# Scratch rows that hold Q and K side by side, and what is zeroed of them at the start

## The reference

```python
xn = _layernorm(x)
# attention branch (attention over the 16 heads of one token, not over tokens)
q = (ln(xn) @ wq + bq).reshape(b, n, 16, 64)          # k, v likewise
fq = elu(q) + 1.0;  fk = elu(k) + 1.0
kv = einsum('bhnd,bhne->bnde', fk, v)
attn = einsum('bhnd,bnde->bhne', fq, kv) / (fq . fk.sum(heads) + 1e-6)
y1 = xn + attn @ wo + bo
s  = y1 + gelu(ln(y1) @ fc_w + fc_b) @ proj_w + proj_b
# routing branch: 64 slots, top-8 softmax weights alpha per token, slot sums over
# the whole sequence, a GRU and slot attention, then out = alpha @ slot values @ wo
g  = silu(route_and_mix(xn))
x  = x + s * g
```

## Time and profile before

| | us |
|---|---|
| median of two timed runs | 2913.88 (2902.56 and 2925.21) |
| profiled execution, device time | 2816.93 |
| its span on the slowest core (core 7) | 2815.4 |
| spans of the other cores | 2774.6 to 2814.9 |

### The profile page before, as it was taken

The page is one execution under the profiler, slowest core; times in us unless marked ns, Lnnn a source line. Parts: engine busy times, 40 slices in busy tenths (PEclk is TensorE's granted clock), DMA queues, the critical chain, the costliest instruction groups (busy, mean ns, idle before and its releaser), DMA issues. The chain is left out here.

```text
span 2815.4 us, 19258 instructions; the slowest of 8 cores (2774.6 to 2815.4 us)
## 1 busy us (share of the span) xinstructions
PE 1251.0 (44%) x6244; PEld 571.1 (20%) x6244; DVE 653.8 (23%) x1713; ACT 376.9 (13%) x594; POOL 119.8 (4%) x133
## 2 busy tenths in 40 slices
PE   0004343443443332173644726430594976849610
PEld 0002121221221110032222322220242433324200
DVE  0023435345343011212314123120102010020022
ACT  0001111211211000010100101000312304122111
POOL 1000000000000001100000000003000010100000
PEclk9997566666665555585866858765697997979855
DMA  9941011111101643443161441529458092762844
GB/s 186 166 72 57 30 60 42 48 60 47 44 30 19 112 72 53 67 80 70 53 105 53 75 74 49 101 67 143 61 54 126 4 118 58 69 81 22 120 172 164
DMA packets 409766, 217.27 MB, mean 77 GB/s; under 512 B 371203, under 2 KB 375428, under 8 KB 409412
## 3 DMA queue, kind: packets, MB, share of 16 engines
q0 software_dynamic: 182176, 89.49, 26.4%
q1 hardware_dynamic: 227492, 126.55, 16.7%
HBM read 230.00 MB, written 58.72 MB: 103 GB/s over the span
## 5 line engine op out<-in xcount | busy, mean ns | idle before, releaser
L578 PE MATMUL pT<-cIDb,xnb 128*128 128x128 bf16 x512 | 64.8, 307 | 258.4 <-DVEq L191 258.4
L590 PE MATMUL pM<-xnTs,w1ab 128*128 128x512 bf16 x512 | 150.6, 463 | 19.9 <-DVEq L191 17.3
L1764 DVE TENSOR_TENSOR y1t<-pTf,y1t 128x512 f32<-128x512 f32 x32 | 22.1, 691 | 579.0 <-PE pTf L1834 579.0
L1803 PE MATMUL pMa<-h2T,fcwb 128*128 128x512 bf16 x512 | 127.7, 394 | 19.1 <-ACTq L191 19.1
L1803 PE MATMUL pMb<-h2T,fcwb 128*128 128x512 bf16 x512 | 124.4, 387 | 0.0
L1820 PE MATMUL pPb<-g1F,pjcb 128*128 128x512 bf16 x512 | 118.8, 392 | 10.6 <-DMA pjcb<-pjw 10.6
L1820 PE MATMUL pPa<-g1F,pjcb 128*128 128x512 bf16 x512 | 113.1, 379 | 9.1 <-ACTq L191 4.7
L578 PEld LDWEIGHTS pT<-cIDb,xnb 128*128 128x128 bf16 x512 | 49.6, 138 | 274.7 <-issue 274.7
L1787 PE MATMUL pT0d<-cIDb,h2b 128*128 128x128 bf16 x128 | 16.2, 307 | 196.6 <-DVEq L191 139.5
L1388 PE MATMUL pBig<-wqb,xhT 128*128 128x512 bf16 x256 | 75.1, 460 | 50.2 <-ACTq L191 50.2
L639 ACT ACT_TABLE_LOAD x16 | 20.5, 1283 | 489.0 <-PE pM L590 489.0
(11 more groups left out here) (250 smaller groups left out, 1790.2 us busy)
## 6 DMA issues: line engine op xcount, KB each, us to landing
xld<-x8k SPq DMA_DIRECT2D x64, 512.0 KB, 5.2
pjcb<-pjw POOLq DMA_DIRECT2D x32, 1024.0 KB, 10.9
y1scr<-XN SPq DMA_DIRECT2D x4, 2048.0 KB, 6.8
y1t<-y1scr SPq DMA_DIRECT2D x4, 2048.0 KB, 10.3
fcwb<-fcw POOLq DMA_DIRECT2D x32, 256.0 KB, 18.9
sscr<-y1t SPq DMA_DIRECT2D x4, 2048.0 KB, 12.7
xre<-x8k SPq DMA_DIRECT2D x16, 512.0 KB, 4.8
sre<-sscr SPq DMA_DIRECT2D x16, 512.0 KB, 5.7
```

What stands on the lines that cost most here:

```text
L578: i = t.transpose(pT0[:, cc * 128:(cc + 1) * 128], xb[:, cc * 128:(cc + 1) * 128], cIDb[:])
L590: i = t.matmul(dstp[:, 0:512], w1ab[:, cc * 512 + ch * 128: cc * 512 + (ch + 1) * 128], xnTs[:, cc * 512:(cc + 1) * 512], start=(cc == 0), ...
L1764: i = v.tensor_tensor(y1v(mt).rearrange("p (s w) -> p s w", s=4)[:, :, d * 128:(d + 1) * 128], pTf[:, :].rearrange("p (s w) -> p s w", s=4 ...
L1803: i = t.matmul(dstp[:, :], fcwb[:, m * 1024 + cc * 128: m * 1024 + (cc + 1) * 128], h2T[:, cc * 512:(cc + 1) * 512], start=(cc == 0), stop ...
```

## The change

1. The two tensors `scr_q` and `scr_k`, (4, 8192, 128) each, become one, `scr_qk`, of 32776 rows of 128 elements. A row holds Q of a token and head in its first 64 elements and K in the other 64. Every half tile of 4096 rows is followed by one spare row.
2. The four copies of zeros become eight of 128 elements each, for the spare rows; `zpad` has 1024 rows.
3. VectorE writes Q and K into `tmb` interleaved by head, 64 elements of one and 64 of the other, and one store carries all 2048 elements of a partition (4096 contiguous bytes). VectorE's first write of a part now waits for that one store of the part before.
4. ScalarE writes V to `AMK` in place of `tmb[:, 0:1024]`, and waits for the store of V of the part before. V's stores count on `ss1`; in `emit_b` VectorE, which is the first to write `AMK` there, waits for the last of them.
5. `FQ2h` is loaded from the start of the rows, `FK2h` from element 64 of the same rows on: what lies in the rows 64 to 127 of the tiles is then no longer zero but K, or Q of the next row. They are not read.

```diff
-        "zpad": np.zeros((32768, 64), dtype=BF),
+        "zpad": np.zeros((1024, 64), dtype=BF),
@@
-    scr_q = nc.dram_tensor("scr_q", [4, 8192, 128], BF16)
-    scr_k = nc.dram_tensor("scr_k", [4, 8192, 128], BF16)
+    scr_qk = nc.dram_tensor("scr_qk", [32776, 128], BF16)
@@ block at L301, GpSimd
-                        for scr in (scr_q, scr_k):
-                            for kk in range(2):
-                                dmx(g, bass.AP(scr, kk * 2097152, [[1, 2097152]]),
-                                    bass.AP(zpad_d.tensor, 0, [[1, 2097152]]),
-                                    swB, 'wB')
+                        for mt4 in range(4):
+                            for half in range(2):
+                                po = (mt4 * 8194 + half * 4097 + 4096) * 128
+                                dmx(g, bass.AP(scr_qk, po, [[1, 128]]),
+                                    bass.AP(zpad_d.tensor, 0, [[1, 128]]),
+                                    swB, 'wB')
@@ emit_a, VectorE
+                            T3 = tmb[:, 0:2048].rearrange("p (h x) -> p h x", h=16)
                             for st in range(4):
                                 v.wait_ge(sac, acS + 3 * st + 1)
-                                if st >= 1:
-                                    v.wait_ge(ss0, s0S + 32 * st)
-                                i = v.scalar_tensor_tensor(
-                                    tmb[:, 0:1024], pBig0[:, :], 1.0, JUNK[:], ...)
+                                v.wait_ge(ss0, s0S + 16 * st)
+                                i = v.scalar_tensor_tensor(
+                                    T3[:, :, 0:64], pBig0 (16 x 64), 1.0, JUNK (16 x 64), ...)
                                 v.wait_ge(sac, acS + 3 * st + 2)
-                                if st >= 1:
-                                    v.wait_ge(ss1, s1S + 16 * st)
-                                i = v.scalar_tensor_tensor(
-                                    tmb[:, 1024:2048], pBig1[:, :], 1.0, JUNK[:], ...)
+                                i = v.scalar_tensor_tensor(
+                                    T3[:, :, 64:128], pBig1 (16 x 64), 1.0, JUNK (16 x 64), ...)
@@ emit_a, ScalarE
-                                a.wait_ge(ss0, s0S + 32 * st + 16)
-                                i = a.activation(tmb[:, 0:1024], pBig0[:, :], AF.Identity)
+                                a.wait_ge(ss1, s1S + 16 * st)
+                                i = a.activation(AMK[:, :], pBig0[:, :], AF.Identity)
@@ emit_a, SyncE, store_st
-                                s.wait_ge(sdv, dvS + 9 + 2 * st)
-                                dmx(s, scr_q [[2048, 128], [128, 16], [1, 64]], tmb[:, 0:1024], ss0, 's0')
                                 s.wait_ge(sdv, dvS + 10 + 2 * st)
-                                dmx(s, scr_k [[2048, 128], [128, 16], [1, 64]], tmb[:, 1024:2048], ss1, 's1')
+                                dmx(s, scr_qk [[2048, 128], [1, 2048]], tmb[:, 0:2048], ss0, 's0')
                                 s.wait_ge(sac, acS + 3 * st + 3)
-                                dmx(s, scr_v ..., tmb[:, 0:1024], ss0, 's0')
+                                dmx(s, scr_v ..., AMK[:, :], ss1, 's1')
@@ transposing loads of both halves
-                                in_=bass.AP(scr_q, ..., [[128, 4096], [1, 128]])   # FQ2h
-                                in_=bass.AP(scr_k, ..., [[128, 4096], [1, 128]])   # FK2h
+                                in_=bass.AP(scr_qk, h, [[128, 4096], [1, 128]])       # FQ2h
+                                in_=bass.AP(scr_qk, h + 64, [[128, 4096], [1, 128]])  # FK2h
@@ emit_b, VectorE
                             v.wait_ge(sld, C['ld'])
+                            v.wait_ge(ss1, s1S)
```

## The result

| us | before | after |
|---|---|---|
| median of the timed runs | 2828.38 (10 runs, lowest 2821.91) | 2692.31 (12 runs, lowest 2680.14) |
| profiled execution (span) | 2816.93 (2815.4) | 2688.01 (2686.5) |
| ratio, 95% interval | | 0.9516 (0.9496 to 0.9536) |

The change is 4.8% faster, 136 us by the medians and 129 us from profiled execution to profiled execution. The median of before moved too: the two runs that were shown ahead of the prediction (2902.56 and 2925.21) turned out to be among the four highest of ten (2883 to 2925), while the other six lie between 2821.91 and 2829.45. In some runs of either kernel the cores of one die show a lower granted clock than the others (0.67 against 0.71 in the changed kernel's run of 2791.91), and the ratios leave these runs out; without them the medians are 2824 and 2687.

The account below looks back on a forecast made before the run. Bound by waits for transfers: zeros before the first barrier, emit_a's stall, emit_b's turn. 93 + 43 - 3 - 3 - 6 = 124 us, taken from the median 2913.88, gives 2790 us; range 2682 to 2825.

Parts of the forecast that it names:

- the same 124: The summed saving of 124 us, subtracted from the median of two timed runs, 2913.88, to give 2790 us.
- stage C: From the first Q matmul of emit_a through the last emit_b and projection; the terms outside the start sum to 31 us.
- The start: At the block at L301, VectorE's first instruction moves from 174.46 to about 81.1 us without the zeros: 93, bounds 78 and 99.
- They cancel: At the start, eight small copies cost about 1.5 us and wvb landing earlier without zeros gains 1.5, leaving 93.
- The stall in `emit_a`: V's copy no longer waits for the store of Q ahead of part 3: 43 us, 34.1 idle and 9 lower clock.
- The margin in part 3: In emit_a, VectorE's Q waits for part 2's joint store but just fits: 0 lost, or 0.8 per tile (-3) with slower transposes.
- VectorE's wait for V's store: In emit_b, VectorE's masks wait until the last V is stored: 0.7 us per tile, -3, range 0 to -6.
- The loads of K: Shifted FK2h loads take 1.5 us longer, counted once per tile at the turn in emit_b: -6, bounds 0 and -12.
- turn: In emit_b, TensorE waits about 20 us per tile for second-half loads and aog's store; a sign expected 20 to 23 us.
- That only the start pays: Rival: emit_a's stall moves to VectorE's Q or K loads lose the gain; 93 + 0 to 15, about 2814, chance 0.24.
- That the zeros weren't what the barrier waited for: Rival: at the start, the barrier did not wait for zeros or wvb lands later; sum 31, 2883 us, chance 0.04.
- The K loads: Rival: two shifted K loads per tile lose 23 us each, or from 16 the kernel is slower at all; chance 0.02.

Follow-up runs that it names:

- V's place alone: The kernel before with only V written to AMK, its store on its own semaphore, and VectorE waiting for the last in emit_b: ratio 0.985, 2794.82 us.
- its repeat: The changed kernel itself, unaltered, timed again on the same chip as the one with unshifted loads of K: ratio 0.957 to the kernel before.
- the first run: The changed kernel with 16 MB of zeros copied again behind wvb in place of the eight small copies: ratio 0.983 to the kernel before.

## Why the prediction was right and wrong

**The time, 2790 forecast, 2692 measured: wrong.** The step that failed is the last of the sum, "I take the same 124 from the median". That median rested on two runs, which ten runs show to be among its four highest, while I had an execution of the same kernel 97 us under both and said that nothing in the trace explained the gap. The other half of that step, 2816.93 - 124 = 2693, is where the changed kernel is: profiled at 2688.01, median 2692.31. The range held that level only because I let it reach down to it. That the sum itself comes so near is in part luck: the start gave 5.6 us more than forecast and stage C 6.1 less. Set against the median that the kernel before really has, my forecast was a change of 38 us, less than a third of what came, although my sum was 124 of the 129 between the two profiled executions.

**The start, 93 forecast, 98.6 measured (97.5 from core 7 to core 5).** The reading was right: the barrier follows the last transfer that GpSimd issued, and moves to the next one. Of the two corrections the one for the eight small copies, 1.5 us, was right. The other was mis-sized, so "They cancel" is the faulty step: without zeros beside it the last piece of `wvb` ended at 73.4 and not at 81.4 (medians of the cores), 8 us earlier where I took 1.5 and bounded at 6. That the barrier follows the last transfer by 1.2 to 1.4 us and not 0.6 takes some of it back.

**The stall in `emit_a`, 43 forecast.** The mechanism was right to the instruction; the tile I had taken apart gained 9.6 us of the 10.0. The size was taken from the core with the longest waits of L1388, 50.2 us. Cores 5 and 2 of the same trace have these rows:

```profile
PE pBig L1388 <- ACTq L191: 40.0, 12, 8.1
...
PE pBig L1388 <- ACTq L191: 45.1, 12, 12.1
```

40.0 is the least of the eight and 45.1 the median. By the same formula, 45.1 - 16.1 = 29 idle and 9 at the lower clock, that is 38. V's place alone shortened stage C by 30.8 over the median of the cores, with its own wait for V's store (about 4) already inside, so 35. Taking one core's waits for all was an error of 5 us; another 3 stay open.

**The margin in part 3.** "It just fits" held: 0.34 us of wait in the tile shown, 1.2 in all on core 5, and 2 on the average of the cores (5.5 at most).

**VectorE's wait for V's store, -3.** It measured about -4: the waits at L1613 are 1.0 to 1.2 us longer than before, four times, and a buffer for V suggests as much.

**The loads of K, -6 and -3.** 0.5 to 0.7 per turn and not 1.5, so -2 to -3, and 0 to -2 in part 3: V's matmuls wait 2.1 us per core for VectorE in the changed kernel, 1.5 in its repeat and 0.5 to 0.9 in the others with shifted loads, against 0.1 to 0.5 with unshifted ones. The choice of the middle between 0 and 3.0 was a guess in want of a row, as said there. Where the prediction says of 3.2 us per load that "the sum would be some 8 us smaller", it counts little but the turn; with part 3, by its own steps, it would be some 14.

**Stage C in all, 31 forecast, 24.9 measured**, 28.4 in the repeat of the changed kernel: a gain about 8 too large, costs together about 4 too large.

**VectorE's strided output at no cost** held: L1351 takes 1.22 to 1.23 us, as L1352 did before. Of the signs listed, four came otherwise: VectorE's first instruction before the window of 79 to 83 us; its masks 1.0 to 1.2 us later and not 0.7; the turn at 19.75 us (79.0 / 4), just under the 20 to 23; and its Q of part 3 shows waits of 10 us for `scr_qk` where I wrote under 2, since the trace puts the whole idle time down to what came last (beyond the 8.4 us that it waits for ScalarE in other parts it is 1.5). None of the signs that would have made it wrong appeared.

**The rivals.** That only the start pays is out: it left stage C 0 to 15 us, where V's place alone took 30.8 from it and the whole change 24.9. That the zeros weren't what the barrier waited for is out by the first run. The K loads do cost, but 0.5 us each and not the 16 from which they would decide.

## What to carry to other kernels

Look for a block or barrier that waits for transfers which nobody inside it reads, and move those behind it: 98 us and another 43 us of this kernel were such waits, with no faster instruction anywhere. A stall at one instruction is often a buffer shared by two values with different readers; giving one of them another place was here worth all that a new layout seemed to bring in that stage. And before a saving in us is taken from a median of two runs, set that median beside the profiled execution: here they were 97 us apart, nearly as much as the whole saving, so the saving and its base are two forecasts. The same saving taken from the profiled execution gave 2693, and 2692 was measured.

## What the runs showed of the hardware

- A load from GpSimd ends very unevenly over the 16 DMA engines: in the changed kernel (core 5) their share falls from full before 66 us to 7% over 72 to 74, one engine's worth, while pieces of `wvb` are still moving, and the barrier falls at 77.0.
- The barrier of a block in which GpSimd issued transfers comes 1.2 to 1.4 us behind the last of them, whoever needs it (the kernel before and the one with one small copy, eight cores each).
- A landing in the trace can be too early where a later transfer adds to the same semaphore: `wvb` by 66.6, while 63 packets of its size moved after 68.
- A transpose load that starts 128 bytes off its 256-byte rows lands about 0.5 us later than the 6.6 to 6.8 us of an unshifted one.
